# Expert gates of a convolution-attention block: the reciprocal deviation from a logarithm and an exponential, and the logits normalised before the two best are found

## What is computed

```python
t = _to_tokens(x + conv(...))            # 32768 tokens of 32 channels
n = (t - mean) / sqrt(var + 1e-5)        # _ln_t
probs = softmax(n @ router_w + router_b) # 8 experts
top_p, top_i = top_k(probs, 2)
top_p = top_p / sum(top_p)               # of the two best, so only their difference counts
expert_out = einsum("bnd,edc->bnec", n, expert_w) + expert_b
t = t + sum_k top_p[k] * expert_out[top_i[k]]
```

## Time and profile before

| | |
|---|---|
| median of 3 runs | 372.4 us (371.52 to 372.99) |
| the profiled execution | 372.87 us, its span 371.0 us |
| PE, VectorE, ScalarE, GpSimd busy | 333.5, 321.3, 276.8, 165.4 us |
| mean granted clock of PE | 0.972 of full |
| table loads on ScalarE | 10, 1.28 us each |

### The profile page before, as it was taken

How to read it: one execution, slowest core, us unless ns; L and a number is a source line. 1 busy time by engine, 2 the same in 40 slices (tenths; PEclk the granted TensorE clock), 3 DMA queues, 4 the chain that set the end, 5 groups by cost and what they waited for, 6 DMA issues and landing times.

```text
span 371.0 us, 12911 instructions
## 1 busy us (share of the span) xinstructions
PE 333.5 (90%) x5496; PEld 176.2 (47%) x5496; DVE 321.3 (87%) x421; ACT 276.8 (75%) x481; POOL 165.4 (45%) x192
## 2 busy tenths in 40 slices
PE   8999888999999979999989989989988997878885
PEld 2556466566566545556555655556542221121221
DVE  1599989998998987999998896899897999999884
ACT  4678768879879885788778897876766788466762
POOL 8520000220220223578535212378658658764663
PEclk9999999999999998999999999999989999687999
DMA  8800010010010000100101101075320856673582
GB/s 299 346 4 3 3 32 11 23 30 18 16 33 29 4 27 7 30 24 10 32 2 31 33 2 32 23 178 117 67 49 29 197 123 129 151 169 86 127 207 96
DMA packets 13386, 26.19 MB, mean 71 GB/s; under 512 B 1681, under 2 KB 3857, under 8 KB 12945
## 3 DMA queue, kind: packets, MB, share of 16 engines
q1 hardware_dynamic: 12752, 23.60, 24.3%
q10 hardware_dynamic: 576, 1.77, 1.2%
HBM read 5.96 MB, written 4.19 MB: 27 GB/s over the span
## 4 chain that ended last, share of the span: by engine, by line
PE 50%; DVE 26%; issue 9%; ACT 8%; DMA 4%; POOL 2%; SPq 0%; POOLq 0%; DVEq 0%; ACTq 0%
PE psum L694 12%; PE psum L713 7%; DVE neg_max L1321 6%; PE psum L679 6%; PE psum L721 4%; PE psum L874 4%; DVE window_work L1324 4%; PE psum L663 4%; PE psum L597 3%; DMA stage<-in_x 2%; DVE window_work L1469 2%; DVE o_tok L1332 2%; DVE probs L1469 2%; PE psum L492 2%; PE psum L864 2%
## 5 line engine op out<-in xcount | busy, mean ns | idle before, releaser
L370 POOL TENSOR_TENSOR o_norm<-o_tok,o_rden 128x128 f32<-128x128 f32 x64 | 24.7, 407 | 155.7 <-DVE o_rden L1334 155.7
L1023 ACT ACTIVATE probs<-psum 128x512 f32<-128x512 f32 x128 | 74.9, 597 | 24.6 <-PE psum L694 23.9
L694 PE MATMUL psum<-weights_sb,window_work 128*128 128x128 f32 x512 | 80.2, 283 | 6.2 <-ACT probs L1023 3.4
L1321 DVE TENSOR_REDUCE neg_max<-psum 128x16 f32<-128x1024 f32 x64 | 76.8, 1199 | 6.3 <-PE psum L679 6.3
L1324 DVE TENSOR_TENSOR window_work<-psum,neg_max 128x1024 f32<-128x1024 f32 x64 | 78.4, 1225 | 2.2
L694 PEld LDWEIGHTS psum<-weights_sb,window_work 128*128 128x128 f32 x512 | 54.7, 140 | 36.8 <-issue 17.5
L713 PE MATMUL psum<-probs,v_cols 128*32 128x64 f32 x2048 | 49.7, 226 | 0.3 <-DVE o_tok L1332 0.3
L713 PEld LDWEIGHTS psum<-probs,v_cols 128*32 128x32 f32 x2048 | 33.7, 111 | 27.8 <-ACT probs L1023 14.1
L1006 ACT ACTIVATE stage<-k_sb,weights_sb 128x512 f32<-128x512 f32 x64 | 44.3, 724 | 0.0
L679 PE MATMUL psum<-stage 32*64 32x256 f32 x1024 | 35.9, 386 | 8.8 <-DVE window_work L1324 6.1
L1332 DVE STREAM_TRANSPOSE o_tok<-psum 128x512 f32<-128x512 f32 x32 | 22.8, 712 | 13.6 <-PE psum L713 13.6
(11 more groups left out here) (148 smaller groups left out, 609.0 us busy)
## 6 DMA issues: line engine op xcount, KB each, us to landing
stage<-act_all SPq DMA_DIRECT2D x36, 256.0 KB, 4.3
out<-v_cols SPq DMA_DIRECT2D x16, 256.0 KB, 2.0
stage<-in_x SPq DMA_DIRECT2D x3, 1024.0 KB, 12.9
x_moved<-x_cur SPq DMA_DIRECT2D x14, 192.0 KB, 2.4
gate_rows<-gate_parts SPq DMA_DIRECT2D x16, 128.0 KB, 3.0
x_moved<-x_cur SPq DMA_DIRECT2D x14, 64.0 KB, 2.2
weights_sb<-weights ACTq DMA_DIRECT2D x1, 811.5 KB, 13.4
stage<-in_x SPq DMA_DIRECT2D x1, 768.0 KB, 5.7
```

The source lines that it names most:

```text
L694: last = nc.tensor.transpose(bank[TURN_BANKS[v % 2]][:, b * P:b * P + P], heads.rearrange("p h k -> p (h k)"), const["c_ident"][:, :])
L1023: nc.scalar.activation(probs[:, w % 4, :], bank[TURN_BANKS[w % 2]][:, :], ACT.Exp).then_inc(exp_done, 1)
L1321: nc.vector.tensor_reduce(m_t, t, AX.X, ALU.max, negate=True).then_inc(max_done, 1)
```

## The change

`token_deviations` takes `exp(-0.5 * ln(var + eps))`, which is `1 / d`, in the layout in which the variances come (tokens in the columns), so the transpose and the reciprocal go. Its Exp counts as step 0. Steps 1 and 2 are now the product of logits and `1 / d` and the addition of the bias, in which the logits are normalised at once; the product of the difference and the one of the probability with `1 / d` go. Step 22 transposes the plain gates straight into `gate_f32`, and step 23, new, multiplies them by `1 / d`, on VectorE for all quads; GpSimd's product goes. There are 28 steps in place of 30. For quads 2 and 3 step 2 is on ScalarE. For quads 0 and 1 it is on GpSimd. The `gates` in the diff is that of VectorE, and of the two `EARLY_STEPS` the first is VectorE's.

```diff
             def token_deviations(quad):
...
-                nc.scalar.activation(std_two[:, quad % 2, :], bank[SHARED][:, :], ACT.Sqrt,
+                nc.scalar.activation(rstd_two[:, quad % 2, :], bank[SHARED][:, :], ACT.Ln,
                                      bias=const["c_eps"][:, 1:2]).then_inc(ln2["std_ready"], 1)
+                act.wait_ge(ln2["std_ready"], quad + (1 + ONE))
+                nc.scalar.activation(rstd_two[:, quad % 2, :], rstd_two[:, quad % 2, :], ACT.Exp, scale=-0.5
+                                     ).then_inc(gate_step[quad], 1)
...
             def gate_copies(quad, step):
+                if step == 2:
+                    one = nc.scalar.activation(spaces[quad].logit, spaces[quad].logit, ACT.Identity,
+                                               bias=const["c_rb"][:, 0:1])
...
             def gates(quad, n):
-                if n == 0:
-                    dve.wait_ge(ln2["std_ready"], quad + (1 + ONE))
-                    one = v.transpose(w.std_t, std_two[:, quad % 2, :])
-                elif n == 1:
-                    one = v.reciprocal(small[:, rden, :], g(w.std_t)[:, :, 0])
-                elif n == 2:
+                if n == 1:
                     dve.wait_ge(raw_done, quad + 1)
-                    one = v.scalar_tensor_tensor(out=w.logit, in0=std_two[:, quad % 2, :], scalar=const["c_rb"][:, 0:1],
-                                                 in1=raw_logits[:, :], op0=ALU.mult, op1=ALU.add)
+                    one = v.tensor_tensor(w.logit, rstd_two[:, quad % 2, :], raw_logits[:, :], ALU.mult)
...
-                elif n == 12:
-                    one = v.tensor_tensor(small[:, gap, :], small[:, near, :], small[:, rden, :], ALU.mult)
...
-                elif n == 19:
-                    one = v.tensor_tensor(small[:, p_best, :], small[:, near, :], small[:, rden, :], ALU.mult)
...
-                elif n == 24:
-                    one = v.transpose(w.rest, w.sum)
+                elif n == 22:
+                    one = v.transpose(gate_f32[:, quad % 2 * CHUNK:(quad % 2 + 1) * CHUNK], w.sum)
+                elif n == 23:
+                    one = v.tensor_tensor(w.rest, gate_f32[:, quad % 2 * CHUNK:(quad % 2 + 1) * CHUNK],
+                                          rstd_two[:, quad % 2, :], ALU.mult)
...
-            EARLY_STEPS = {(6, 8): (0, 1), (7, 8): (3, 4), (8, 1): (7,), (8, 8): (10,), (9, 1): (15,),
-                           (9, 8): (17, 18, 19, 20), (10, 1): (24,)}
+            EARLY_STEPS = {(7, 8): (3, 4), (8, 1): (7,), (8, 8): (10,), (9, 1): (14,), (9, 8): (16, 17, 18), (10, 1): (22, 23)}
...
-            EARLY_STEPS = (((), (2,)), ((5, 6), (8, 9)), ((11, 12, 13, 14), (16,)), ((21, 22, 23), (26, 27)), ((29,), ()))
+            EARLY_STEPS = (((), (1, 2)), ((5, 6), (8, 9)), ((11, 12, 13), (15,)), ((19, 20, 21), (25,)), ((27,), ()))
...
-        LATE_EXP = {EARLY: 8, EARLY + 1: 17}
+        LATE_EXP = {EARLY: 8, EARLY + 1: 16}
```

More of the change, by code:

```diff
@@ L255, in __init__ @@
                 self.mask1 = at[3]
-                self.std_t, self.rest = std_pair[:, quad % 2, :], std_pair[:, quad % 2, :]
+                self.rest = std_pair[:, quad % 2, :]
         spaces = [Gates(quad) for quad in range(QUADS)]
-        best, second, best_rank, second_rank, gap, e_gap, total, p_best, p_second, rden, near = range(11)
+        best, second, best_rank, second_rank, gap, e_gap, total, p_best, p_second = range(9)
         rank8 = const["c_rank"][:, :].unsqueeze(1).to_broadcast([P, CHUNK // E, E])
@@ L1382, in gates @@
                 elif n == 11:
-                    one = v.tensor_tensor(small[:, near, :], small[:, second, :], small[:, best, :], ALU.subtract)
+                    one = v.tensor_tensor(small[:, gap, :], small[:, second, :], small[:, best, :], ALU.subtract)
                 elif n == 12:
-                    one = v.tensor_tensor(small[:, gap, :], small[:, near, :], small[:, rden, :], ALU.mult)
-                elif n == 13:
                     one = v.tensor_tensor(g(w.a), g(w.rest), wide(second), ALU.is_equal)
+                elif n == 14:
+                    one = v.tensor_reduce(small[:, second_rank, :], g(w.b), AX.X, ALU.max)
@@ L1388, in gates @@
                 elif n == 15:
[L1389 removed]
+                    one = v.tensor_tensor(g(w.mask2), g(w.b), wide(second_rank), ALU.is_equal)
                 elif n == 16:
[L1391 to L1392 removed]
                     dve.wait_ge(gate_exp, quad + 1)
                     one = v.tensor_scalar(small[:, total, :], small[:, e_gap, :], 1.0, None, ALU.add)
+                elif n == 17:
+                    one = v.reciprocal(small[:, p_best, :], small[:, total, :])
@@ L1395, in gates @@
                 elif n == 18:
-                    one = v.reciprocal(small[:, near, :], small[:, total, :])
-                elif n == 19:
-                    one = v.tensor_tensor(small[:, p_best, :], small[:, near, :], small[:, rden, :], ALU.mult)
+                    one = v.tensor_tensor(small[:, p_second, :], small[:, e_gap, :], small[:, p_best, :], ALU.mult)
                 elif n == 20:
-                    one = v.tensor_tensor(small[:, p_second, :], small[:, e_gap, :], small[:, p_best, :], ALU.mult)
+                    one = v.tensor_tensor(g(w.b), g(w.mask2), wide(p_second), ALU.mult)
@@ L1457, in steps @@
                     for n in late_steps(quad, 2 * c + eh):
-                        if n not in LATE_POOL[quad] and n not in (25, 28):
+                        if n not in LATE_POOL[quad] and n not in (2, 24, 26):
                             gates(quad, n)
```

77 lines of the change are left out of this document (31 added, 46 removed).

## The result

The change makes the kernel slower: 381.4 us median of 4 runs (378.27 to 382.13) against 372.7 of 4 runs of the kernel before, ratio 1.0216, 95% interval 1.0146 to 1.0285. The forecast was 377.0 and its range ended at 380.3. The direction was right, and the loss is twice the forecast one. The profiled execution took 382.08 us, its span is 380.1 and the mean granted clock 0.967 (before 372.87, 371.0 and 0.972).

The account below looks back on a forecast made before the run. No engine is full; PE (90%) and VectorE (87%) come near, and at chunk 6 ScalarE is on the path. 3.2 + 1.6 - 1.2 + 0.3 - 0.6 + 0.35 + 1.0 = +4.65: 377.5 profiled, 377.0 us median, range 373.2 to 380.3.

Parts of the forecast that it names:

- Attention stage as a whole: Chunks 6 to 15 before the expert stage: the chunk terms and the clock term together, +3.65 us.
- Chunk 6: ScalarE gets two loads and one Exp more, all on the path, +3.2 us; a clock fall behind PE's wait, +1.6.
- Chunk 9: VectorE has one small product less; the remaining one starts ahead of GpSimd's residual, -1.2 us.
- Chunk 10: VectorE's new product with the reciprocal, 0.68 us or more, where PE leads: +0.3, bounds 0 and 1.0.
- Chunk 12: ScalarE has 0.6 us more, VectorE drops 1.2 of transpose and reciprocal behind the wait for PE: -0.6.
- Chunk 15: ScalarE has 0.6 us more before the last exponentials, small product partly saved: +0.35, bounds -0.5 and 0.8.
- Expert stage: Later ScalarE at half 9 and two copies at half 11 against less VectorE work: +1.0 us, bounds -2.5 and +3.5.
- From there to the last gate step VectorE has less, about -1.5: Expert stage after half 11: VectorE work moved earlier, to ScalarE or dropped, one product added, about -1.5 us.
- The end of that stage: Quad 3's last gate step sets the expert stage's end, through SyncE's queue to chunk 13; up to 1.06 us good.
- D: Rival: clock falls more often or longer, in chunk 7 and at halves 13 to 19; 380.2 us, chance 0.13.
- E: Rival: each of three added loads empties ScalarE and holds it as long again; 380.8 us, chance 0.03.
- F: Rival: Ln and Exp share one table; 1.28 us less at chunks 6, 12, 15, half 9; 369.3, chance 0.02.

Follow-up runs that it names:

- grouped: Changed kernel with the instance deviation of chunk 6 taken as a logarithm too, in order Ln, Ln, Exp, Exp, two loads fewer: 376.02 us, 1.0085.
- before_extra_exp: Kernel before plus a spare, unused Exp behind each square root of the token deviations, 12 loads, VectorE and GpSimd work as before: 382.43 us.
- after_both: Changed kernel, 12 loads, quad 3's Exp behind the logits copy, gate steps of quads 2 and 3 later, four of quad 3 on GpSimd: 380.19 us.
- one_table: Changed kernel with one table for Ln and Exp loaded once, second instance deviation as exp(0.5 ln), 2 loads in place of 12: 370.38 us.
- after_exp_behind: Changed kernel with, at half 9, the logits copy right behind Ln and quad 3's load and Exp behind that copy: 382.14 us.
- after_places: Changed kernel, still 12 loads, with most late gate steps of quads 2 and 3 one half later, about where the kernel before had them: 384.62 us.
- one_table_pool: Changed kernel with one table, gate steps of quads 2 and 3 later, four of quad 3 on GpSimd, chunk 13's tokens ahead of gate rows: 366.89 us.
- after_deferred: Changed kernel with every Exp of the deviations moved away from its Ln to where ScalarE is not waited for, 11 loads: 377.5 us.

## Why the prediction was right and wrong

- **Attention stage as a whole, +3.65**: +5.17, and +5.04, +4.88 and +3.85 in three other kernels with the same instructions up to there. Right in the main; how far it is off hangs on the clock of the execution.
- **Chunk 6, +3.2 and +1.6 for the clock** (bounds 3.2 to 5.7): +5.54. Right in mechanism. `current(8)` came 4.98 later, the clock fell for some 4 us behind the 4.57 us and once more behind 2.44; I had counted one further stretch of 3.3 us. *grouped* confirms that the place is worth more than the length of its loads.
- **Chunk 9, -1.2**: -1.39, of which 1.10 at the chunk's end, by the step named. The remaining small product no longer runs beside GpSimd's residual.
- **Chunk 10, +0.3**: +0.04 net; the 0.8 us that it costs in mid-chunk is made good in the same chunk, since PE leads there.
- **Chunk 12, -0.6**: +0.53, wrong in sign. The step that failed is that a fall of the clock was put at nothing here. Three kernels take the sum apart. *before_extra_exp*, with the load and Exp and without the saving, loses 0.54 at full clock, as the 0.6 of the prediction had it. *after_both*, the same instructions as the change here and full clock, gains 0.25, so VectorE's saving is worth about 0.8 of the 1.2 forecast (it then waits 0.17 for PE). In the change the same wait of PE, 1.55 us for `probs` (1.01 before), was followed by half clock, the product behind it took 1.77 (1.12 before), and the fall cost the other 0.8. VectorE's wait, the 2.75 of the earlier trace rows, is 4.01 in the change and 3.29 in *after_both*; under each stands the stretch of the clock:

```profile
231.62 0.72 DVE L1333 STREAM_TRANSPOSE o_tok<-psum 128x512 f32<-128x512 f32 x1 [4.01 <-PE psum L708]
229.00:231.00 2.00, 2.00 (x10) 0.87 (x12) 0.00 (x0) 1.82 (x4) 0.00 (x0) 0.50 0.31 90
```

```profile
230.22 0.72 DVE L1339 STREAM_TRANSPOSE o_tok<-psum 128x512 f32<-128x512 f32 x1 [3.29 <-PE psum L708]
229.00:231.00 2.00, 1.74 (x48) 1.38 (x52) 0.75 (x2) 2.00 (x5) 0.00 (x0) 1.00 0.44 131
```

- **Chunk 15, +0.35**: +0.46.
- **Expert stage, +1.0** (bounds -2.5 and +3.5): +3.84, the largest miss and outside its bound. Three of its parts failed. "PE's idle 1.35 grows to about 3" was right (2.87), but the price of what follows was not 1.0: *before_extra_exp* shows 3.0 at half 11 from this alone. "From there to the last gate step VectorE has less, about -1.5" failed: in the change step 23 runs beside GpSimd's products at 1.78 and 1.32 us in place of 0.68, and steps 20 and 21 of quad 3 at 1.25 and 1.65 in place of 0.70 and 0.69, and *one_table* shows 3.0 us at half 11 from VectorE's side alone. And I had put a lighter VectorE against a later ScalarE as a sum, where they are two chains that meet at the same half: either makes PE stand, and to take one away gave nothing (*after_exp_behind*, +0.7 us; *after_places*, +3.2). Part of the +3.84 is also a difference of two executions, as the kernel before has its falls of the clock at other halves.
- **The end of that stage**: the last gate step came 8.1 us later (at 352.49 against 344.36), and VectorE's wait for the tokens of chunk 13 grew from the 1.06 of the earlier trace rows to 2.53. As forecast, the end hangs on that step; it moved in the bad direction by 1.5 us.

Of the rivals, D (more falls of the clock, 380.2) describes best what happened, though only the one in chunk 7 lies where it was expected. E, that a load empties the engine, comes out near the total (380.8; 381.1 by the figure of the Trainium skill, "ScalarE: Activation LUTs", section "What ACT_TABLE_LOAD costs"), and is wrong all the same: in the timeline above every function starts 0.02 us or less after its load ends, and the instruction ahead of a load ends where the load begins. A total that fits is no evidence for a mechanism. It also counts three added loads where the kernel has two more (12 for 10): the one at half 9 is moved there from ahead of the next Exp. F was 2 in 100 as a fact of this kernel, and what it would give (369.3) is near what the one-table kernel does (370.4), but by luck: F takes away 4 loads, that kernel has 10 fewer than the change, its attention stage gains 5.65 us where F's terms give about 1.8, and its expert stage loses 3.59 where F has a gain.

A third chain was not in the prediction at all: ScalarE's gate copy of half 10, behind load and Exp, and GpSimd behind the copy (*after_both*). Open is the share of each wait in the expert stage. The traces have their long PE waits at different halves (11, 12, 17, 20 or 24), and no run took all away.

## What to carry to other kernels

Before you trade VectorE work for ScalarE work, look at what waits for ScalarE at that very place: four Exps with their loads cost 9 to 10 us directly behind Ln or Sqrt, and the whole saving on VectorE was worth 0 to 1. Where a function needs another table, first look whether one set holds all the functions of the stage, and ask for it by name; here that was worth 11 us to the change and 2.5 to 3 to the kernel before. In a ring of engines that is already in step, don't add up gains and losses of two engines that meet at one point, and give a wait of PE a second price for the clock that may fall behind it: here it fell behind some waits of 1.2 to 2 us and not behind others, so that price is a range.

## What the runs showed of the hardware

- **VectorE is held by GpSimd.** A 128x512 product of VectorE with both inputs in SBUF takes 0.68 us alone and 0.99, 1.29, 1.66, 1.76 or 1.78 beside a GpSimd product, and each of these ends 0.54 or 0.55 after GpSimd's. The transpose at 302.75 in *one_table* (0.71, one SBUF input) and the products with one input in PSUM (0.67 to 0.69) are not held; such a product in the kernel before, and GpSimd's around it:

```profile
312.61 1.73 POOL L460 TENSOR_TENSOR window_work<-stage,q_sb 128x512 f32<-128x512 f32 x1
313.12 0.67 DVE L1466 TENSOR_TENSOR window_work<-stage,psum 128x512 f32<-128x512 f32 x1
```

The Trainium skill, "SBUF — State Buffer", section "SBUF: two separate sides", says the same: the two engines share a pair of ports, locked for a whole instruction by a VectorE operation with two SBUF inputs against a GpSimd one that reads SBUF. The traces agree; they also show GpSimd's own product at 1.72 and 1.73 in place of 1.28 where it began during a product of VectorE, and at 1.26 where it began first.
- **Alike waits, other clocks.** Ahead of the queries of chunk 8 PE stood for 1.93 us in *one_table*, and the clock was 0.60 and 0.54 in the four microseconds from 139; in *one_table_pool* it stood for 2.04 and the clock stayed full:

```profile
139.00:141.00 2.00, 2.00 (x36) 0.65 (x40) 1.75 (x2) 0.42 (x1) 0.00 (x0) 0.60 0.00 0
141.00:143.00 2.00, 2.00 (x46) 1.83 (x36) 0.91 (x2) 0.85 (x2) 0.00 (x0) 0.54 0.00 0
```

```profile
139.00:141.00 2.00, 1.99 (x67) 1.05 (x52) 1.72 (x3) 1.07 (x2) 0.00 (x0) 1.00 0.00 0
141.00:143.00 2.00, 2.00 (x30) 0.96 (x35) 0.79 (x2) 1.83 (x5) 0.77 (x2) 1.00 0.03 8
```

- **Slower executions are those with a lower clock.** Runs of one kernel order themselves nearly by it: *after_deferred* took 374.3, 375.5, 376.5, 378.5 and 379.8 us at mean clocks of 0.976, 0.977, 0.971, 0.966 and 0.962. Which of the two makes the other is not shown. A difference of 1 us between two kernels with a few runs each is therefore not told as a gain here.
